# Two attention heads' row maxima: from three PSUM banks in turn and one reduction a head, to two fixed banks and one reduction for both

## The reference

```python
x = x + _layernorm(attn(_layernorm(x)))          # x: (2, 2048, 128) float32
q, k, v = (einsum('bsd,dhk->bshk', xn, W) + b for W, b in ...)      # 16 heads of 64
attn = softmax(einsum('bqhd,bkhd->bhqk', q / sqrt(64), k))          # over all 2048 keys
out  = einsum('bqhd,hdm->bqm', einsum('bhqk,bkhd->bqhd', attn, v), Wo) + bo
x = x + _layernorm(ffn(_layernorm(x)))           # rank 32, width 512
```

## Time and profile before

| | us |
|---|---|
| median of three runs | 2409.32 (2408.78 to 2409.55) |
| the profiled execution's own time | 2408.61 |
| its span in the trace | 2406.8 |
| TensorE busy | 2363.3 (98%) |
| ScalarE busy | 2140.5 (89%) |
| VectorE busy | 2044.8 (85%) |
| GpSimd busy | 2033.3 (84%) |

### The profile page before, as it was taken

One profiled execution on the slowest core, in us unless ns is written; L12 is line 12 of the kernel. 1 busy time (PEld: TensorE's weight loads), 2 busy tenths in 40 slices (PEclk: granted clock), 3 DMA queues, 4 the chain that ended last, 5 costly groups with the idle time before them and its releaser, 6 DMA issues.

```text
span 2406.8 us, 44126 instructions
## 1 busy us (share of the span) xinstructions
PE 2363.3 (98%) x15628; PEld 1158.0 (48%) x15628; DVE 2044.8 (85%) x3249; ACT 2140.5 (89%) x2427; POOL 2033.3 (84%) x1141
## 2 busy tenths in 40 slices
PE   6999999999999999999999999999999999999998
PEld 3444444445445454444445444454444545444444
DVE  7888888888888888888888888888888888888977
ACT  5999999898998999999998999999999998989976
POOL 4888888888888888888888888888888888889986
PEclk8999999999999999999999999999999999999999
DMA  1100001000000000100001000100000000110101
GB/s 51 28 15 28 28 15 33 28 14 28 28 20 28 28 14 28 34 15 27 28 15 33 28 15 27 33 21 22 28 27 21 28 27 15 35 29 21 36 27 36
DMA packets 62973, 62.59 MB, mean 26 GB/s; under 512 B 28868, under 2 KB 46660, under 8 KB 62756
## 3 DMA queue, kind: packets, MB, share of 16 engines
q1 hardware_dynamic: 61748, 59.44, 8.3%
q10 hardware_dynamic: 1008, 0.33, 0.1%
HBM read 56.88 MB, written 2.61 MB: 25 GB/s over the span
## 4 chain that ended last, share of the span: by engine, by line
PE 92%; DVE 3%; POOL 2%; ACT 2%; issue 1%; DMA 0%; POOLq 0%; ACTq 0%; DVEq 0%
PE o_ps L428 35%; PE spare_ps L390 13%; PE score_ps L407 11%; PE score_ps L410 9%; PE score_ps L413 9%; PE spare_ps L376 3%; PE spare_ps L367 3%; PE spare_ps L358 3%; PE spare_ps L473 3%; POOL total L1113 2%; PE spare_ps L440 1%; DVE max_part L838 1%; ACT probs L664 1%; ACT score_ps L654 0%; DVE ln_stats L804 0%
## 5 line engine op out<-in xcount | busy, mean ns | idle before, releaser
L1113 POOL TENSOR_TENSOR total<-total,probs 128x832 f32<-128x832 f32 (+1 forms) x896 | 1761.9, 1966 | 294.1 <-ACT probs L664 216.9
L838 DVE TENSOR_REDUCE max_part<-spare_ps 128x1 f32<-128x512 f32 x2027 | 1302.2, 684 | 310.5 <-PE spare_ps L390 294.4
L664 ACT ACTIVATE probs<-score_ps 128x1024 f32<-128x1024 f32 x1024 | 993.7, 1023 | 219.1 <-PE score_ps L413 217.0
L654 ACT ACTIVATE score_ps<-m_all 128x1024 f32<-128x1024 f32 x1024 | 1012.1, 1032 | 14.4 <-DMA m_all<-m_scratch 14.4
L428 PE MATMUL o_ps<-probs,v_sb 128*64 128x512 f32 x4096 | 974.9, 597 | 0.0
L428 PEld LDWEIGHTS o_ps<-probs,v_sb 128*64 128x64 f32 x4096 | 271.5, 137 | 423.5 <-issue 278.3
L390 PE MATMUL spare_ps<-k_hi,q_hi 64*128 64x512 f32 x2027 | 455.8, 445 | 11.7 <-DVE max_part L838 8.3
L407 PE MATMUL score_ps<-q_hi,k_hi 64*128 64x512 f32 x2048 | 426.9, 413 | 1.2 <-ACT score_ps L654 1.2
L413 PE MATMUL score_ps<-q_hi,k_lo 64*128 64x512 f32 x2048 | 405.3, 391 | 0.0
L410 PE MATMUL score_ps<-q_lo,k_hi 64*128 64x512 f32 x2048 | 404.7, 391 | 0.0
L390 PEld LDWEIGHTS spare_ps<-k_hi,q_hi 64*128 64x128 f32 x2027 | 194.1, 184 | 424.4 <-issue 239.8
(11 more groups left out here) (131 smaller groups left out, 926.4 us busy)
## 6 DMA issues: line engine op xcount, KB each, us to landing
m_all<-m_scratch SPq DMA_DIRECT2D x64, 512.0 KB, 4.3
denom<-denom_scratch SPq DMA_DIRECT2D x122, 128.0 KB, 2.9
m_scratch<-neg_rows SPq DMA_DIRECT2D x256, 1.0 KB
y_acc<-in_L_attn_x SPq DMA_DIRECT2D x8, 256.0 KB, 5.9
xg<-in_L_attn_x SPq DMA_DIRECT2D x8, 256.0 KB, 2.8
block_out<-probs SPq DMA_DIRECT2D x8, 256.0 KB, 2.3
denom_col<-denom SPq DMA_DIRECT2D x61, 4.0 KB
denom_scratch<-denom_col SPq DMA_DIRECT2D x61, 4.0 KB, 1.4
```

Of the source, the lines that this page charges most:

```text
L654: nc.scalar.activation(score_ps[st % 2][:], m_all[:, G % 2], ACT.Copy).then_inc(s["seed_done"], 1)
L664: nc.scalar.activation(probs[:, st % RING], score_ps[st % 2][:], ACT.Exp, scale=SCALE).then_inc(s["exp_done"], 1)
L838: nc.vector.reduce_max(max_part[:, G % 2, h, qt, kc:kc + 1], bank[max_bank(n, h)], AX.X).then_inc(s["max_done"], 1)
L1113: nc.gpsimd.tensor_tensor(others(total[:, G % 2], G), so_far, others(probs[:, st % RING], G), ALU.add).then_inc(s["sum_done"], 1)
```

## The change

In the doubles, `spare_banks()` now gives every maxima pair `r0` (head 0) and `r1` (head 1). Everything else goes to `r2`, except that the two halves of the last head projections take `r0` and `r1`. `dve_max` handles a pair in one `reduce_max` where its two banks lie side by side, with a 128 x 2 x 512 input and two columns of output, and adds 2 to `max_done`. The first 22 pairs keep their banks; 21 of them are side by side too, and one (`o`,`r2`) keeps two reductions.

```diff
@@ spare_banks()
     def use(*key):
-        out[key] = f"r{len(out) % 3}"
+        out[key] = "r2"
...
             for h in range(2 if st < STEPS else 0):
-                use("max", 2 * st + h)
+                out["max", 2 * st + h] = f"r{h}"
...
         if n in HEADS_AT:
-            use("Wo0", HEADS_AT[n])
-            use("Wo1", HEADS_AT[n])
+            out["Wo0", HEADS_AT[n]] = "r0"
+            out["Wo1", HEADS_AT[n]] = "r1"
@@ build()
-        def dve_max(dve, n, h):
+        def dve_max(dve, n):
+
             G, qt, kc = max_step(n)
             dve.wait_ge(s["max_ready"], n + 1)
-            if n % T == 0 and h == 0 and G >= 2:
+            if n % T == 0 and G >= 2:
                 dve.wait_ge(s["neg_max_done"], G - 1)
-            nc.vector.reduce_max(max_part[:, G % 2, h, qt, kc:kc + 1], bank[max_bank(n, h)], AX.X).then_inc(s["max_done"], 1)
+            pair = max_bank(n, 0), max_bank(n, 1)
+            both = {("r0", "r1"): spare_ps[:, 0:2, :], ("s00", "s01"): score_ps[0][:], ("s10", "s11"): score_ps[1][:]}
+            if pair in both:
+                nc.vector.reduce_max(max_part[:, G % 2, :, qt, kc], both[pair], AX.X).then_inc(s["max_done"], 2)
+            else:
+                for h in range(2):
+                    nc.vector.reduce_max(max_part[:, G % 2, h, qt, kc:kc + 1], bank[pair[h]], AX.X).then_inc(s["max_done"], 1)
@@ dve_program()
                 if more:
-                    dve_max(dve, 2 * n + LEAD, 0)
-                    dve_max(dve, 2 * n + LEAD, 1)
+                    dve_max(dve, 2 * n + LEAD)
...
                 if more:
-                    dve_max(dve, 2 * n + LEAD + 1, 0)
-                    dve_max(dve, 2 * n + LEAD + 1, 1)
+                    dve_max(dve, 2 * n + LEAD + 1)
```

More of the change, by code:

```diff
@@ L1018, in dve_program @@
             for n in range(LEAD):
-                for h in range(2):
-                    dve_max(dve, n, h)
+                dve_max(dve, n)
                 if n == T - 1:
```

## The result

The changed kernel takes 2588.35 us (median of 4 runs) against 2409.07: 1.0750 times the time before, 95% interval 1.0737 to 1.0763. The forecast was 2534, range 2485 to 2580. The direction and the place were right. The size was 54 us short, 8 us outside the range. In the table further down, one of the eleven executions of *before, merge at B only* took 3666 us at a granted clock of 0.58; its ratio leaves that one out.

A forecast was written before the change was run, and what follows sets the result against it. TensorE was taken to bound the kernel. Waits of 1.13 us plus weight loads of 0.88 made 2.01 us a chunk, +126 us over 62.6 chunks, less 1 in the opening: from 2408.6 to 2533.6, forecast 2534, range 2485 to 2580.

The forecast's parts named there:

- TensorE bounds, and pair B waits for both maxima of A: In the doubles: TensorE, 98% busy, sets the time; B reuses A's banks, so its wait adds 1.13 us a chunk.
- The third bank's other users cost nothing in `r2`: Other work moved into `r2`: its pieces never meet closely, the tightest gap being 1.25 us, so the cost is nothing.
- The merged reduction takes 1.22 us: On VectorE: one reduction over 1024 columns takes 1.22 us against 1.29 for two; bounds 1.07 to 1.29.
- The 0.15 a pair: On VectorE: saving per merged pair by the skill's rule about emptying the pipe; the prediction already doubted that size.
- The uncovered weight load, 0.11 after a B that waits: On TensorE: a waiting B holds the engine 0.11 us longer, 0.88 us a chunk; bounds 0 and 0.12.
- From the last maximum to TensorE, and VectorE's start after A: Hand-overs around the reduction: B starts 0.10 us after the maxima end; where VectorE is free, maxima start 0.54 after A.
- The sum over d: A to B in a chunk's eight doubles: grows by 0.05 to 0.29 us each, 1.13 us a chunk.
- VectorE's busy time: Sign in the trace after: VectorE's busy time falls by about 150 us, 0.15 for each of 1023 pairs.
- The weight load isn't hidden: Rival at pair B: TensorE loads weights while waiting, so only 1.13 us a chunk stays, 2479 us; chance 0.08.
- `r2` is no queue: Rival in `r2`: denominators let go too late make K wait; half a us once a chunk gives 2565; chance 0.05.
- The clock didn't fall: Rival on TensorE: short waits bring the lower clock for a tenth of the time, 2770 us; chance 0.03.
- A reduction under 0.93 us: Rival on VectorE: the merged reduction is so short that nothing waits, leaving 2408 us; chance 0.04.

The follow-up runs named there:

- before, merge at B only: Kernel before, three banks in turn, one reduction for both heads only in the opening's first 22 pairs and at pairs B with neighbouring banks; 2411.06 us, ratio 1.0004.
- Half width: Changed kernel with a single TensorE wait per pair, the reduction adding 1 and reading only the first 256 of 512 columns per bank; 2402.03 us, ratio 0.9974.
- merge alone: Kernel before with its three banks in turn, but one reduction for both heads where a pair's banks are neighbours; 2523.48 us, ratio 1.0476.
- count by one: Changed kernel, but the merged reduction adds 1 to max_done instead of 2 and all waits count pairs; 2555.97 us, ratio 1.0610.
- one wait: Changed kernel, but TensorE waits once for a maxima pair instead of once for each head's bank; 2549.46 us, ratio 1.0583.
- banks alone: Changed kernel's fixed banks, but two reductions a pair, each adding 1, as before the change; 2603.36 us, ratio 1.0808.
- cover at chosen places: Changed kernel with a single TensorE wait per pair, reductions adding 1, TensorE's other work ahead of pair B at d = 0, 4, 6, 7 after the first unit; 2527.58 us.

## Why the prediction was right and where it failed

*TensorE bounds, and pair B waits for both maxima of A.* Right in the main. Half width takes the wait away and gets the time before; merge alone brings it back in the 333 doubles where pair A is merged, for 115 us. That VectorE's work is free before the change was a little too simple: at d = 6 and 7 the projection behind B already waited for a maximum.

*The third bank's other users cost nothing in `r2`.* Right: half width keeps those banks.

*The merged reduction takes 1.22 us.* Right: 1.224. By the Trainium skill (VectorE: DVE Perf Modes, The TRN2 errata) the estimate was 1.19; the row decides. The 0.15 a pair that the prediction worked out by the Trainium skill (VectorE: DVE Perf Modes, The DRAIN you can't avoid) isn't borne out: 1.29 became 1.22. That section was read too widely: it adds that a next operation that is not held (its word for one that must wait until all before it have finished) starts earlier. The trace agrees, with two reductions of 0.68 in 1.29.

*The uncovered weight load, 0.11 after a B that waits.* The size was right (0.43 to the next matmul, was 0.32). The cause was stated too narrowly: a pair has it also when it waits for nothing but stands behind K.

*From the last maximum to TensorE, and VectorE's start after A.* This step failed. The mechanism was right; these two terms of the distance from A to B were too small. I took 0.10 and 0.54 from pairs of the old kernel. In the changed kernel they are 0.15 and 0.60 to 0.61. In all some 0.11 us in 501 doubles, 56 us; the miss was 54. VectorE's part is the addition of 2: the wait leaves the reduction and stands ahead of it (961 rows at line 836), and counting by one gives 32 us back. TensorE's part is two waits for one pair: with one wait the hand-over is 0.05, which gives 39 us back. VectorE's cost had no row to be read from: no instruction of the old chunk added 2 to a semaphore. TensorE's had one. The old opening's 18th pair waits for the maxima alone, and starts 0.15 behind their end (34.80 + 1.27 = 36.07), with a row of line 335 at 36.1. It stands in the stretch of lower clock of the earlier trace rows, but has the chunk's value. The pair of the earlier trace rows that I took 0.10 from waits for K too.

```profile
34.80 1.27 DVE L838 TENSOR_REDUCE max_part<-score_ps 128x1 f32<-128x512 f32 x2
...
36.22 0.80 PE L390 MATMUL score_ps<-k_hi,q_hi 64*128 64x512 f32 x2 [0.61 <-DVE max_part L838]
```

I gave these terms no bounds; 0.05 more on the hand-over alone would have taken the upper end from 2580 to 2605.

*The sum over d.* Right in its pattern: A to B at d = 6 grew by 0.39 (0.27 forecast plus that 0.11), at d = 4 by 0.26 (0.14 plus 0.11). From pair A of d = 5 to that of d = 7 it takes 9.29 us (1317.47 to 1326.76), 9.08 forecast; two times 0.11 is missing. A slip without weight is in the upper bound: 0.07 us in 501 doubles is 35 us, not 37.

*VectorE's busy time.* I forecast 150 us less; it is 67 (2044.8 to 1977.7). The two old reductions overlapped, and overlapping time counts once. The 0.07 of the latency term was the right number here too.

*The rivals.* The weight load isn't hidden, and `r2` is no queue: the list of waits of the changed kernel has no projection behind the doubles' maxima. The clock didn't fall. The windows of 100 to 500 and of 1000 to 1500 us both show a granted clock of 1.00; the first of them, in the columns of the earlier trace rows:

```profile
100.00:500.00 400.00, 387.52 (x2482) 184.00 (x2478) 305.92 (x309) 337.84 (x378) 316.02 (x168) 1.00 0.08 23
```

The Trainium skill's warning (TensorE: Matmul & The Clock Gate, A second HAM failure mode) that a cycle through banks, with TensorE idle between groups, makes the clock swing does not show here, with TensorE busy 97% of that window. A reduction under 0.93 us would indeed cost nothing: the one of 0.69 costs nothing.

## What to carry to other kernels

When two buffers used in turn become one that is waited for as a whole, compare the time from a pair's start to its release (start, operation, hand-over) with the work that stands before the next write, place by place; an instruction saved on an engine that waits is worth nothing by itself, and here what it took to save it cost 7.5%. Count the hand-over as part of the operation: give an instruction one wait, and let the producer add 1, wherever nothing covers the wait. Moving other work into the gap pays only if what it displaces, on both engines, has cover too.

## What the runs showed of the hardware

- A reduction that adds 2 to a semaphore has its wait ahead of it as an instruction of its own (961 rows against none) and starts 0.07 us later behind the pair it waits for than the same reduction adding 1: 0.61 against 0.54, the medians at d = 4 of the changed kernel and of *count by one*. In the old kernel the same edit makes 0.61 of 0.54.
- TensorE's first matmul follows the end of the maxima by 0.05 us with one wait (*one wait*) and by 0.14 to 0.15 with two waits for the same semaphore (changed kernel); it makes no difference whether the first of the two was fulfilled 0.6 us before (*banks alone*). It is 0.10 in the 30 doubles in which the pair waits for K too.
- A matmul pair behind the K projection has an uncovered weight load also when it waits for nothing: 0.43 us to the next matmul (*cover at chosen places*), 0.32 behind the scores (before). Pairs A, behind the value products, show it in VectorE's start: 0.54 behind A, 0.43 behind B.
